# Thirteen turns of normed rows in the second pass: DMA transposes of two-byte halves in place of TensorE transposes

## The chip, the cores and the metric

One NeuronCore of a Trainium2 chip runs the whole kernel. The metric is the device time of one execution in microseconds (us); lower is better. The kernel before takes 807.27 us (median of three runs, 802.72 to 809.95).

## What is computed

Sixteen sequences x of 256 rows and 256 columns are updated by a gated cross-attention layer (a residual feed-forward network, a causal long convolution taken from a context, and a second feed-forward network) and then by a mixture of 16 experts on heads of 32 columns, two experts per head. Cut to what matters here:

```
y   = ffn(x_normed, W1a, W1b) * conv(context)        # "first pass", then the gate
xr  = ffn(y, W2a, W2b)                               # ffn(v) = silu(norm(v) @ Wa + ba) @ Wb + bb + v
x   = x + tanh(g_xattn) * xr                         # "second pass"
h   = norm(x) @ Wm + bm                              # heads
out = x + tanh(g_ffn) * (top2_experts(softmax(h @ E), h) @ Wo + bo)
```

## The kernel before

The 4,096 rows are eight blocks of 512 (b = 0 to 7); a block is a tile of 128 partitions by 1024 floats. Each engine has a program written out by hand, in which instructions run in order; they meet by semaphores alone. SyncE (SP) issues every DMA, in one queue, in program order. Products are made from f16 high and low parts (h, l), three products for one (`THREE`), into fp32 in PSUM.

A matrix product needs the columns of its rows on the partitions, so each block of normed rows is **turned** before use: eight TensorE transposes of 128x128 fp32 through the identity `ID` into two PSUM banks (`turn`, L554), then ScalarE rounds each bank to f16 into `XT[t % 2]["h"]` (L1427) and VectorE subtracts for the low part (`turn_lo`, L897). There are 24 turns: t = 0 to 7 of the first pass, `turn2(b)` of the gated rows and `turn3(b)` of the rows after the second network. `turn2(b)` for b of 2 and more uses `XT[0]`, `turn3(b)` for b up to 5 uses `XT[1]`.

The **second pass** is a loop over stages s = 0 to 7 in all programs. In stage s TensorE runs, in this order: `layer2` of block s-1 (50 matmuls, L590 and L598; its k-th quarter waits for the low part that GpSimd makes of the silu, L1610); `third_turn(s-2)`; `layer1` of block s (24 matmuls, L581); `logits` of block s-3 (L684); `heads` of block s-2 (12 matmuls, L673); `gated_turn(s+1)`. ScalarE runs the norm of block s-2 (`third_norm`, L1458 into DC), the norm of block s+1 (`gated_norm`, L1458 into `XN` in WK), the high part of turn3, eight silus (L1435, L1438), the high part of the heads (L1452) and the high part of turn2. VectorE makes the low parts, the norms' statistics (L914 to L940, which wait for a power by GpSimd, L1604), the residual sums (L1111, L1117: `second_out`), the logits less their maximum (L1128, L1131) and, in stages 4 to 7, fourteen steps that choose the experts of block 0 (`ROUTE0`).

SP's queue in a stage: one load of x (L333, which waits for `second_out` of block s-1), then `spread_heads(s-2)`: 12 DMAs of 64 KB that copy the heads to the layout of the experts (4 of the low part, L430, which wait for `heads_lo` of VectorE; 8 of the high part, L435). After stage 7 the experts' loop begins: 256 iterations to the end of the kernel. Its weights go to memory and come back (`keep_weights`, L447; `spread_weights`, L458), behind `spread_heads(5)` in SP's queue.

Of the kernel before, what the change touches and what calls it, by code (L numbers as in the profile page):

```python
# [64 lines left out]

def norm2(b):

    return 8 + b if b < 2 else 6 + 2 * b
# [21 lines left out]
def transposer_uses():  # L90

    out = [("conv", 0, 0), ("conv", 0, 1)]
    out += [("turn", turn2(s), k) for s in range(3) for k in range(2)]
    for s in range(2, NB):
        out += [("turn", turn3(s - 2), k) for k in range(2)]
        out += [("head", s - 2, g) for g in range(2)]
# [20 lines left out]
def flamingo_kernel(nc, xd, ctxT, peT, wp1, wp2, win, w1a, w1b, w2a, w2b, wm, wo,  # L117
                    ew1, ew2, eb, cols, rows, ident, ramp, tvec, ones, out):
    with ExitStack() as ctx:
# [79 lines left out]
        late_turns = [turn2(b) for b in range(3, NB)]  # L199

        def pt(kind, i, k):
            if kind == "turn" and i == 0:
                return PB[:, 512 * k:512 * k + 512]
            if kind == "turn" and i < NB:
                k += 0 if i < 5 else 2
                return PA[:, 512 * k:512 * k + 512]
            if kind == "turn" and i in late_turns:
                return PA[:, 512 * k:512 * k + 512]
# [51 lines left out]
        s_tl = [sem(f"s_tl{b}") for b in range(NB)]  # L260
        s_zx = [sem(f"s_zx{u}") for u in range(4)]
        s_out = [sem(f"s_out{u}") for u in range(2)]
        s_wt = [sem(f"s_wt{b}") for b in range(NB)]
# [9 lines left out]
        v_n3, v_hi, v_hh, v_cl = (sem("v_" + n) for n in ("n3", "hi", "hh", "cl"))  # L273
        a_exp, a_gelu = (sem("a_" + n) for n in ("exp", "gelu"))
# [15 lines left out]
        def pt_freed(kind, i, k):  # L290
            return {"turn": (v_lo, 2 * i + k + 1), "conv": (v_dc, NC),
# [5 lines left out]
        def xt_freed(t):  # L297
# [3 lines left out]
            for b in range(NB):  # L301
                if t == turn2(b):
                    return p_l1, 4 * (8 + b) + 4
                if t == turn3(b):
                    return p_head, 2 * b + 2

# [22 lines left out]
        def sync_program(sp):  # L329
# [107 lines left out]

            for s in range(NB):
                if s >= 1 and s + 1 < NB:
                    sp.wait_ge(v_out, 8 + s)  # L440
                    load_x(1, s + 1)
                if s >= 2:
                    spread_heads(s - 2)

            def keep_weights(b):
                sp.wait_ge(v_wt, b + 1)
                sp.dma_start(wtd.ap()[b, :, :], weighed(b)).then_inc(s_wt[b], 16)  # L447

            def spread_weights(m):
# [4 lines left out]
                if e == 0 and g == 0:  # L454
                    sp.wait_ge(s_wt[b], 16)
# [10 lines left out]
            keep_weights(0)  # L466
            for m in range(4):
# [20 lines left out]
        def tensor_program(pe):  # L488
# [51 lines left out]
            def turn(t, src):  # L540
                for k in range(2):
                    if t in late_turns:
                        bank = pt("turn", t, k)
                        pe.wait_ge(a_silu, 4 * (8 + late_turns.index(t) + 2) + k + 1)
                    elif t >= NB:
# [21 lines left out]
            def layer1(j, t, w):  # L567
                pe.wait_ge(v_lo, 2 * t + 2)
# [82 lines left out]
            def gated_turn(b):  # L651
                pe.wait_ge(a_n2, b + 1)
                turn(turn2(b), XN)

            def first_gated():
                gated_turn(0)
# [9 lines left out]
            def heads(b):  # L666
                t = turn3(b)
                xt = XT[t % 2]
                pe.wait_ge(v_lo, 2 * t + 2)
# [66 lines left out]
            for s in range(NB):  # L736
# [5 lines left out]
                if s >= 2:  # L742
# [1020 lines left out]
```

## Time and profile before

| what | value |
|---|---|
| median of three runs | 807.27 us |
| profiled execution, its span | 807.5 us |
| TensorE busy | 774.8 us, 96% |
| ScalarE busy | 670.3 us, 83% |
| VectorE busy | 531.4 us, 66% |
| GpSimd busy | 496.0 us, 61% |
| all DMAs | 117.06 MB, mean 145 GB/s |

The span is that of the one execution that was profiled; it lies 0.2 us above the median. A busy share is an average over stages that have different limits: the first pass ends near 190 us, the second pass near 300 us, and the rest is the experts' loop.

### The profile page before, as it was taken

How to read it: one execution, taken by the hardware profiler on the slowest of the kernel's cores; microseconds unless marked ns; L12 is line 12 of the kernel's file. 1: busy time of each engine (PE TensorE's matmuls, PEld its weight loads, DVE VectorE, ACT ScalarE, POOL GpSimd, SP SyncE). 2: the span in 40 equal slices, each digit the busy share in tenths (PEclk: the TensorE clock that was granted, in tenths of full speed). 3: DMA queues.
4: the chain of work that ended last, by engine and by line, in shares of the span. 5: the costliest groups of instructions: out<-in, count | busy, mean ns of one | idle time of the engine just before them, and what ended most of it. 6: DMA issues, size and time to landing. Idle time of an engine off the chain costs nothing.

```text
span 807.5 us, 23892 instructions
## 1 busy us (share of the span) xinstructions
PE 774.8 (96%) x9972; PEld 380.7 (47%) x9972; DVE 531.4 (66%) x988; ACT 670.3 (83%) x840; POOL 496.0 (61%) x389
## 2 busy tenths in 40 slices
PE   9999788889999998998999999999999999999997
PEld 4667455646676664333334434434434433434433
DVE  5999854557688985684665664764764764664445
ACT  4465854445869878799999999999999999999995
POOL 1374332027753542585787787787787787787674
PEclk9999999979999999999999999999999999999999
DMA  8990699941133316655465554555555555465552
GB/s 291 219 244 28 135 187 191 198 107 36 50 86 89 89 44 166 156 143 149 145 158 151 166 157 147 159 170 146 157 159 151 165 159 155 148 171 158 149 154 67
DMA packets 85971, 117.06 MB, mean 145 GB/s; under 512 B 13123, under 2 KB 65475, under 8 KB 85764
## 3 DMA queue, kind: packets, MB, share of 16 engines
q1 hardware_dynamic: 85864, 115.55, 55.2%
q8 instruction: 78, 1.28, 0.7%
q14 instruction: 29, 0.24, 0.1%
HBM read 101.28 MB, written 6.94 MB: 134 GB/s over the span
## 4 chain that ended last, share of the span: by engine, by line
PE 71%; DVE 10%; ACT 7%; SPq 5%; issue 3%; DMA 2%; POOL 2%; POOLq 0%; DVEq 0%; ACTq 0%
PE PB L792 26%; PE PA L780 18%; PE PT L780 9%; PE PA L581 5%; SPq L345 4%; PE PB L598 3%; PE PB L814 2%; PE PA L535 2%; DMA RA<-wpd 2%; DVE WK L897 2%; DVE SM L914 1%; ACT WK L1458 1%; PE PT L673 1%; ACT WK L1438 1%; ACT WK L1435 1%
## 5 line engine op out<-in xcount | busy, mean ns | idle before, releaser
L1677 POOL TENSOR_TENSOR WK<-WK 128x512 f32<-128x512 f32 x238 | 320.3, 1346 | 112.3 <-DVE WK L1333 102.2
L1582 ACT ACTIVATE WK<-PA 128x1024 f32<-128x1024 f32 x349 | 360.1, 1140 | 10.8 <-PE PA L780 10.3
L792 PE MATMUL PB<-WK,EW 128*32 128x512 f32 x2040 | 264.7, 594 | 0.4 <-DVE WK L1333 0.4
L780 PE MATMUL PA<-RA,EW 98*32 98x512 f16 x2800 | 201.6, 380 | 0.5 <-ACT WK L1582 0.5
L1582 ACT ACTIVATE WK<-PT 128x1024 f32<-128x1024 f32 x163 | 187.1, 1148 | 2.0 <-PE PT L780 1.7
L1610 POOL TENSOR_TENSOR WK<-WK 128x512 f16<-128x512 f32 x64 | 79.5, 1255 | 129.9 <-ACT WK L1438 128.6
L780 PEld LDWEIGHTS PA<-RA,EW 98*32 98x32 f16 x2800 | 68.1, 95 | 154.9 <-issue 80.4
L780 PE MATMUL PT<-RA,EW 98*32 98x512 f16 (+1 forms) x1312 | 99.6, 379 | 4.8 <-ACT WK L1582 3.4
L792 PEld LDWEIGHTS PB<-WK,EW 128*32 128x32 f32 x2040 | 62.4, 111 | 52.3 <-DVE WK L1333 0.9
L1333 DVE SCALAR_TENSOR_TENSOR WK<-PB,CV,W2h 128x512 f32<-128x512 f32 x64 | 48.1, 751 | 49.1 <-PE PB L792 49.1
L1333 DVE SCALAR_TENSOR_TENSOR WK<-PB,CV,W2l 128x512 f32<-128x512 f32 x63 | 47.3, 751 | 44.3 <-PE PB L792 44.3
L1333 DVE SCALAR_TENSOR_TENSOR WK<-PB,CV,DC 128x512 f32<-128x512 f32 x64 | 47.8, 748 | 37.1 <-PE PB L792 36.7
L780 PEld LDWEIGHTS PT<-RA,EW 98*32 98x32 f16 x1312 | 32.5, 95 | 76.9 <-issue 35.7
L1333 DVE SCALAR_TENSOR_TENSOR WK<-PB,CV,W1h 128x512 f32<-128x512 f32 x64 | 47.7, 746 | 29.0 <-PE PB L792 29.0
L1435 ACT ACTIVATE WK<-PA,CV 128x512 f16<-128x512 f32 x64 | 44.1, 690 | 24.6 <-PE PA L581 23.9
L1604 POOL TENSOR_TENSOR SM<-SM 128x4 f32<-128x4 f32 (+1 forms) x24 | 33.2, 1385 | 40.5 <-DVE SM L927 22.5
L1438 ACT ACTIVATE WK<-PA,CV 128x512 f32<-128x512 f32 x64 | 44.2, 690 | 0.0
L598 PE MATMUL PB<-W1h,WK 128*128 128x256 f16 x256 | 42.5, 273 | 1.0 <-issue 1.0
L598 PE MATMUL PB<-W2h,WK 128*128 128x256 f16 x256 | 42.5, 273 | 0.9 <-POOL WK L1610 0.9
L581 PE MATMUL PA<-WK,W1h 128*128 128x512 f16 x128 | 38.7, 384 | 0.0
L581 PE MATMUL PA<-WK,W2h 128*128 128x512 f16 x128 | 38.1, 379 | 0.0
L1080 DVE TENSOR_REDUCE DC<-PB 128x256 f32<-128x512 f32 x28 | 19.2, 691 | 26.6 <-PE PB L638 26.6
(220 smaller groups left out, 1086.8 us busy)
## 6 DMA issues: line engine op xcount, KB each, us to landing
RA<-wpd SPq DMA_DIRECT2D x128, 134.1 KB, 5.8
W1h<-wtd SPq DMA_DIRECT2D x128, 128.0 KB, 2.7
DC<-wtd SPq DMA_DIRECT2D x128, 128.0 KB, 2.8
W2h<-wtd SPq DMA_DIRECT2D x128, 128.0 KB, 2.7
W2l<-wtd SPq DMA_DIRECT2D x128, 128.0 KB, 2.7
WK<-in_x SPq DMA_DIRECT2D x15, 512.0 KB, 4.0
RA<-DC SPq DMA_DIRECT2D x96, 64.0 KB, 2.0
out<-WK SPq DMA_DIRECT2D x16, 256.0 KB, 2.8
```

The lines of the kernel that those rows point to most:

```text
L345: sp.dma_start(slot(c)[p0:p0 + K1, :, :, :].rearrange("p q i n -> p (q i) n"), src).then_inc(l_T[c % TR], 16)
L581: m = pe.matmul(pa, w[a][:, 512 * k + 128 * n:512 * k + 128 * n + 128], xt[b][:, 512 * k:512 * k + 512], start=(i == 0), stop=(i == 5))
L598: m = pe.matmul(o[t], S[b][:, 512 * k + 128 * t:512 * k + 128 * t + 128], w[a][:, 1024 + 256 * k:1024 + 256 * k + 256], start=False, stop= ...
L780: m = pe.matmul(pre(k)[32 * j:32 * j + 32, w * q:w * q + w], EW1[0:98, 128 * e + 32 * j:128 * e + 32 * j + 32], TS[0:98, h, t0:t0 + w], st ...
L792: m = pe.matmul(o[32 * q:32 * q + 32, :], EW2[:, 32 * e:32 * e + 32], hb[:, 512 * q:512 * q + 512], start=True, stop=True)
L1333: ve.scalar_tensor_tensor(out=dst, in0=po("down", n), scalar=col(C_B2 + e), in1=WB[n // 2 % 4][:, 512 * (n % 2):512 * (n % 2) + 512], op0= ...
L1435: ac.activation(S["h"][:, 512 * n:512 * n + 512], pa, ACT.Silu, scale=1.0 / SC, bias=col(bcol + n))
L1438: ac.activation(SF[n], pa, ACT.Silu, scale=1.0 / SC, bias=col(bcol + n)).then_inc(a_silu, 1)
L1582: ac.activation(HB[n % NH][:, 1024 * p:1024 * p + 1024], pre(k)[:, :], ACT.Gelu, scale=1.0 / (SC * SC)).then_inc(a_gelu, 1)
L1604: po_.tensor_tensor(SM[:, o:o + n], SM[:, o:o + n], SM[:, 6:7].broadcast_to([128, n]), ALU.pow).then_inc(g_pow, 1)
L1610: po_.tensor_tensor(sl, SF[n], sh, ALU.subtract).then_inc(g_slo, 1)
L1677: po_.tensor_tensor(AC[g], AC[g], PR[m % 3], ALU.add).then_inc(g_ac, 1)
```

## The change

Of the 24 turns, 13 go by another way: `turn2(1)` to `turn2(7)` and `turn3(0)` to `turn3(5)`. TensorE no longer transposes them. ScalarE rounds the normed rows themselves to f16 (`gated_hi` into `GN`, `third_hi` into `TN3`, 128x1024 each), VectorE subtracts for the low part (`gated_lo`, `third_lo`, 128x1024 each), and SP issues one `dma_start_transpose` of the 128 x 2048 two-byte elements (512 KB), which writes high and low parts of the turned block to `XT[t % 2]` (`turn_rows`). `layer1` and `heads` wait for that DMA's semaphore. The transpose waits on SP for the low part and for the last reader of that `XT`. VectorE's order changes with it, `third_norm(6)` moves behind `heads(5)` on ScalarE, and six semaphores are saved elsewhere (`s_wt`), which changes no order of work.

```diff
+        GN = WK[:, 5120:6144].bitcast(F16)
+        TN3 = W1["h"]
...
+            def turn_rows(t, rows, count, done):
+
+                sp.wait_ge(count, done)
+                sp.wait_ge(*xt_freed(t - 2))
+                both = WK[:, 3072 + 1024 * (t % 2):4096 + 1024 * (t % 2)].bitcast(F16)
+                sp.dma_start_transpose(both.rearrange("p (j n) -> p j n", n=128), rows[:, :]).then_inc(s_xt[t % 2], 16)
+
             for s in range(NB):
+                if s >= 2:
+                    turn_rows(turn3(s - 2), TN3, v_g3, s - 1)
                 if s >= 1 and s + 1 < NB:
                     sp.wait_ge(v_out, 8 + s)
                     load_x(1, s + 1)
+                if s + 1 < NB:
+                    turn_rows(turn2(s + 1), GN, v_g2, s + 1)
                 if s >= 2:
                     spread_heads(s - 2)
...
             def layer1(j, t, w):
-                pe.wait_ge(v_lo, 2 * t + 2)
+                if NB < t:
+                    pe.wait_ge(*turned(t))
+                else:
+                    pe.wait_ge(v_lo, 2 * t + 2)
                 xt = XT[t % 2]
...
-                if s >= 2:
-                    third_turn(s - 2)
...
-                if s + 1 < NB:
-                    gated_turn(s + 1)
...
+            def gated_lo(b):
+                ve.wait_ge(a_g2, b)
+                ve.tensor_tensor(by_halves(GN[:, 1024:2048]), XN.rearrange("p (t k c) -> p t k c", k=2, c=128),
+                                 by_halves(GN[:, 0:1024]), ALU.subtract).then_inc(v_g2, 1)
+
+            def third_lo(b):
+                ve.wait_ge(a_g3, b + 1)
+                ve.tensor_tensor(by_halves(TN3[:, 1024:2048]),
+                                 WSP[:, 1024 * b:1024 * b + 1024].rearrange("p (t k c) -> p t k c", k=2, c=128),
+                                 by_halves(TN3[:, 0:1024]), ALU.subtract).then_inc(v_g3, 1)
...
             for s in range(NB):
-                if s >= 1:
-                    turn_lo(turn2(s))
-                    if s + 1 < NB:
-                        gated_stats(s + 1)
-                        norm_shift(norm2(s + 1))
+                if 1 <= s < NB - 1:
+                    gated_stats(s + 1)
+                    norm_shift(norm2(s + 1))
                 for i in ROUTE0.get(s, ()):
                     route(0, i)
+                if s >= 2:
+                    third_lo(s - 2)
                 if s >= 1:
                     second_out(s - 1)
-                if s >= 2:
-                    turn_lo(turn3(s - 2))
-                if s >= 1:
                     third_stats(s - 1)
+                if s + 1 < NB:
+                    gated_lo(s + 1)
                 second_sum(s)
                 if s >= 3:
                     less_max(s - 3, PB[:, 0:512])
-                if s == 7:
-                    norm_shift(norm3(6))
+                if s >= 1:
+                    norm_shift(norm3(s - 1))
                 if s >= 2:
                     heads_lo(s - 2)
-                if 1 <= s < 7:
-                    norm_shift(norm3(s - 1))
...
+            def gated_hi(b):
+
+                if b == 1:
+                    ac.wait_ge(v_eb, 1)
+                else:
+                    ac.wait_ge(*turned(turn2(b - 1)))
+                ac.wait_ge(a_n2, b + 1)
+                split_rows(XN, GN[:, 0:1024], a_g2)
+
+            def third_hi(b):
+
+                if b:
+                    ac.wait_ge(*turned(turn3(b - 1)))
+                ac.wait_ge(a_n3, b + 1)
+                split_rows(WSP[:, 1024 * b:1024 * b + 1024], TN3[:, 0:1024], a_g3)
...
                 if s >= 2:
                     third_norm(s - 2)
+                    third_hi(s - 2)
                 if s == 5:
                     exp(0)
                     exp(1)
                 if s + 1 < NB:
                     gated_norm(s + 1)
-                if s >= 2:
-                    turn(turn3(s - 2))
+                    gated_hi(s + 1)
                 layer1(8 + s, C_B2A)
                 if s >= 2:
                     heads(s - 2)
-                if s + 1 < NB:
-                    turn(turn2(s + 1))
-                else:
-                    third_norm(6)
+            third_norm(6)
 
             def gelu(k):
                 n, p = divmod(k, 2)

```

Three places in the program show the new orders. First SP's queue around stage 4 (names in brackets are the semaphores waited for: v_hl and a_hh the heads' parts, v_g2 and v_g3 the low parts of the normed rows, p_l1 and p_head the last readers of `XT`). Before:

```order
L333 DMA WK<-in_x 128x4x256 [waits v_out]
L430 DMA RA<-DC 32x2x512 [waits v_hl]
L430 DMA RA<-DC 32x2x512 x3
L435 DMA RA<-DC 32x2x512 [waits a_hh]
L435 DMA RA<-DC 32x2x512 x7
```

Of the change:

```order
L444 DMA RA<-DC 32x2x512 [waits v_hl]
L444 DMA RA<-DC 32x2x512 x3
L449 DMA RA<-DC 32x2x512 [waits a_hh]
L449 DMA RA<-DC 32x2x512 x7
L457 DMA_TRANSPOSE WK<-W1h 128x16x128 [waits p_head,v_g3]
L347 DMA WK<-in_x 128x4x256 [waits v_out]
L457 DMA_TRANSPOSE WK<-WK 128x16x128 [waits p_l1,v_g2]
```

The transpose of block s-2 (source `TN3`, in W1h) stands behind the 12 DMAs of block s-3's heads; that of block s+1 (source `GN`, in WK) stands behind the load of x.

Second, VectorE in stage 4, from the experts' steps of the stage to the logits. Before:

```order
L1151 SCALAR_TENSOR_TENSOR W1l<-W1l,DC 128x512 [waits v_rt]
L1117 SCALAR_TENSOR_TENSOR XR<-PB,SM,WK 128x1024 [waits v_sum,p_l2]
L897 TENSOR_TENSOR WK<-PT,WK 128x512 [waits a_hi] x2
L914 BN_STATS SM<-XR 128x6 [waits a_n2,v_out]
L914 BN_STATS SM<-XR 128x6 x3
L921 BN_AGGR SM<-SM 128x2 [waits v_st]
L921 BN_AGGR SM<-SM 128x2 x3
L927 TENSOR_SCALAR SM<-SM 128x4 [waits v_ag]
L1111 SCALAR_TENSOR_TENSOR WK<-XR,SM,WK 128x1024 [waits l_x10]
```

Of the change:

```order
L1187 SCALAR_TENSOR_TENSOR W1l<-W1l,DC 128x512 [waits v_rt]
L931 TENSOR_TENSOR W1h<-DC,W1h 128x4x2x128 [waits a_g3]
L1153 SCALAR_TENSOR_TENSOR XR<-PB,SM,WK 128x1024 [waits v_sum,p_l2]
L950 BN_STATS SM<-XR 128x6 [waits a_n2,v_out]
L950 BN_STATS SM<-XR 128x6 x3
L957 BN_AGGR SM<-SM 128x2 [waits v_st]
L957 BN_AGGR SM<-SM 128x2 x3
L963 TENSOR_SCALAR SM<-SM 128x4 [waits v_ag]
L926 TENSOR_TENSOR WK<-WK 128x4x2x128 [waits a_g2]
L1147 SCALAR_TENSOR_TENSOR WK<-XR,SM,WK 128x1024 [waits l_x10]
```

The low part of turn3 moves ahead of `second_out`, and that of turn2 comes behind the statistics of the stage before instead of at the start of its own.

Third, TensorE between `layer2` and `layer1` of stage 5. Before, the end of `layer2`, turn3 and the first rows of `layer1`:

```order
L598 MATMUL PB<-W2h,WK 128x256 x2
L598 MATMUL PB<-W2l,WK 128x256
L554 MATMUL PT<-ID,DC 128x128 x8
L581 MATMUL PA<-WK,W2h 128x512 x2
L581 MATMUL PA<-WK,W2l 128x512
```

Of the change:

```order
L624 MATMUL PB<-W2h,WK 128x256 x2
L624 MATMUL PB<-W2l,WK 128x256
L607 MATMUL PA<-WK,W2h 128x512 x2
L607 MATMUL PA<-WK,W2l 128x512
L607 MATMUL PA<-WK,W2h 128x512 x2
```

The eight transposes are gone, here and behind `heads`; nothing takes their place on TensorE.

## Rows read from the trace of the kernel before

**Rows 1.** The page: span, TensorE's row, the chain that ended last.
```profile
span 807.5 us, 23892 instructions
PE 774.8 (96%) x9972; PEld 380.7 (47%) x9972; DVE 531.4 (66%) x988; ACT 670.3 (83%) x840; POOL 496.0 (61%) x389
PE 71%; DVE 10%; ACT 7%; SPq 5%; issue 3%; DMA 2%; POOL 2%; POOLq 0%; DVEq 0%; ACTq 0%
```
**Rows 2.** Windows of 16 us: from:to, length, engines' busy us, TensorE's clock, DMA share, GB/s.
```profile
236.00:252.00 16.00, 15.92 (x127) 10.96 (x128) 14.61 (x35) 11.73 (x23) 7.70 (x7) 1.00 0.31 84
268.00:284.00 16.00, 15.91 (x127) 10.73 (x124) 14.71 (x36) 12.52 (x24) 7.90 (x7) 1.00 0.32 83
```
**Rows 3.** Chain of waits from 236 to 300 us: start, us, engine, line; stage 7.
```profile
284.23 0.59 PE PB L590 x2
284.82 5.24 PE PB L598 x48
290.06 0.87 PE PT L554 x8
290.93 5.18 PE PA L581 x24
296.11 0.70 PE PB L684 x24
296.81 2.60 PE PT L673 x12
```
**Rows 4.** Timeline of TensorE: start, us, line, tiles, count; first `heads(0)`, last `heads(5)`.
```profile
216.20 0.38 PE L673 MATMUL PT<-WK,WMh 128*128 128x512 f16 x1
...
296.65 0.38 PE L673 MATMUL PT<-WK,WMh 128*128 128x512 f16 x1
```
**Rows 5.** Timeline of SP's queue, stages 3, 5 and 7 into the experts' loop.
```profile
229.75 0.59 SPq L333 DMA_DIRECT2D WK<-in_x  x1
...
253.11 2.51 SPq L430 DMA_DIRECT2D RA<-DC  x4
255.66 5.07 SPq L435 DMA_DIRECT2D RA<-DC  x8
260.77 0.59 SPq L333 DMA_DIRECT2D WK<-in_x  x1
...
300.94 2.50 SPq L430 DMA_DIRECT2D RA<-DC  x4
303.48 5.07 SPq L435 DMA_DIRECT2D RA<-DC  x8
308.59 0.58 SPq L447 DMA_DIRECT2D wtd<-DC  x1
```
**Rows 6.** DMA issues from 205 to 315 us: KB each, median us to landing.
```profile
RA<-DC SPq DMA_DIRECT2D x72, 64.0 KB, 2.0
WK<-in_x SPq DMA_DIRECT2D x5, 512.0 KB, 3.8
```
**Rows 7.** The page: DMA queue (packets, MB, share), slowest issue per byte.
```profile
q1 hardware_dynamic: 85864, 115.55, 55.2%
RA<-wpd SPq DMA_DIRECT2D x128, 134.1 KB, 5.8
```
**Rows 8.** Groups of instructions: busy us, mean ns of one, idle before.
```profile
L1072 DVE TENSOR_TENSOR RA<-DC,RA 128x1024 f16<-128x1024 f32 x4 | 5.7, 1456 | 0.8 <-ACT RA L1514 0.8
L1514 ACT ACTIVATE RA<-DC 128x1024 f16<-128x1024 f32 x4 | 4.1, 1054 | 5.8 <-DVE DC L1062 5.8
```
**Rows 9.** Timelines of ScalarE and VectorE: `third_norm(0)`; both turns' low parts in stage 5.
```profile
207.43 2.08 ACT L1458 ACTIVATE DC<-XR,SM 128x256 f32<-128x256 f32 x4 [0.96 <-DVE SM L940]
...
253.49 1.28 DVE L897 TENSOR_TENSOR WK<-PA,WK 128x512 f16<-128x512 f32 x2
...
260.67 1.29 DVE L897 TENSOR_TENSOR WK<-PT,WK 128x512 f16<-128x512 f32 x2 [0.90 <-ACT WK L1427]
```
**Rows 10.** Windows of 1 us, columns as in rows 2: clock around TensorE's idle times.
```profile
160.00:161.00 1.00, 0.33 (x25) 0.36 (x32) 0.40 (x1) 0.00 (x0) 0.00 (x0) 1.00 1.11 208
...
309.00:310.00 1.00, 0.00 (x0) 0.00 (x0) 1.00 (x2) 0.98 (x2) 0.00 (x0) 1.00 0.57 178
310.00:311.00 1.00, 0.82 (x3) 0.36 (x4) 1.00 (x4) 0.99 (x2) 0.00 (x0) 0.76 0.40 150
311.00:312.00 1.00, 1.00 (x4) 0.30 (x3) 0.93 (x7) 1.00 (x2) 0.00 (x0) 0.50 0.12 33
```
**Rows 11.** Timeline of TensorE: an idle time of 1.0 us; `heads(6)` from its first matmul on.
```profile
160.67 0.63 PE L624 MATMUL PT<-RA 60*32 60x256 f16 x32 [1.00 <-DMA RA<-wpd]
...
310.18 0.73 PE L673 MATMUL PT<-WK,WMh 128*128 128x512 f16 x2 [1.73 <-DVE WK L897]
...
314.56 0.61 PE L780 MATMUL PA<-RA,EW 98*32 98x512 f16 x8
```

More of the change, by code:

```diff
@@ L63, in turn3, with by_tensor, by_transfer @@
     return norm3(b)
+def by_tensor(t):
+    return (*range(NB), turn2(0), 22, 23).index(t)
+def by_transfer(t):
+    ts = [turn2(b) for b in range(1, NB)] + [turn3(b) for b in range(6)]
+    return sorted(u for u in ts if u % 2 == t % 2).index(t)
 def norm2(b):
@@ L92, in transposer_uses @@
     out = [("conv", 0, 0), ("conv", 0, 1)]
[L93 to L96, printed above, removed]
+    out += [("turn", turn2(0), k) for k in range(2)]
+    out += [("head", b, g) for b in range(6) for g in range(2)]
     out += [("wt", 0, 0), ("turn", 22, 0), ("turn", 22, 1), ("head", 6, 0), ("head", 6, 1),
@@ L197, in flamingo_kernel @@
         po_at = {u: i for i, u in enumerate(po_list)}
-        late_turns = [turn2(b) for b in range(3, NB)]
+        GN = WK[:, 5120:6144].bitcast(F16)
+        TN3 = W1["h"]
         def pt(kind, i, k):
@@ L205, in pt @@
                 k += 0 if i < 5 else 2
-                return PA[:, 512 * k:512 * k + 512]
-            if kind == "turn" and i in late_turns:
                 return PA[:, 512 * k:512 * k + 512]
@@ L260, in flamingo_kernel @@
         s_tl = [sem(f"s_tl{b}") for b in range(NB)]
+        s_xt = [sem(f"s_xt{i}") for i in range(2)]
         s_zx = [sem(f"s_zx{u}") for u in range(4)]
         s_out = [sem(f"s_out{u}") for u in range(2)]
-        s_wt = [sem(f"s_wt{b}") for b in range(NB)]
+        s_wt = [sem(f"s_wt{i}") for i in range(2)]
         l_wb = [sem(f"l_wb{i}") for i in range(4)]
@@ L273, in flamingo_kernel @@
         v_n3, v_hi, v_hh, v_cl = (sem("v_" + n) for n in ("n3", "hi", "hh", "cl"))
+        a_g2, a_g3, v_g2, v_g3 = (sem(n) for n in ("a_g2", "a_g3", "v_g2", "v_g3"))
         a_exp, a_gelu = (sem("a_" + n) for n in ("exp", "gelu"))
@@ L290, in pt_freed @@
         def pt_freed(kind, i, k):
-            return {"turn": (v_lo, 2 * i + k + 1), "conv": (v_dc, NC),
+            return {"turn": (v_lo, 2 * by_tensor(i if kind == "turn" else 0) + k + 1), "conv": (v_dc, NC),
                     "head": (v_hl, 2 * i + k + 1), "wt": (v_wt, 1)}[kind]
@@ L466, in sync_program @@
             keep_weights(0)
+            sp.wait_ge(*turned(turn3(5)))
             for m in range(4):
@@ L541, in turn @@
                 for k in range(2):
[L542 to L545, printed above, removed]
+                    if t >= NB:
                         bank = take_pt("turn", t, k)
@@ L649, in convs @@
                         flip(c, s)
-            def gated_turn(b):
-                pe.wait_ge(a_n2, b + 1)
-                turn(turn2(b), XN)
             def first_gated():
-                gated_turn(0)
+                pe.wait_ge(a_n2, 1)
+                turn(turn2(0), XN)
             def third_turn(b):
@@ L668, in heads @@
                 xt = XT[t % 2]
[L669 removed]
+                if b < 6:
+                    pe.wait_ge(*turned(t))
+                else:
+                    pe.wait_ge(v_lo, 2 * by_tensor(t) + 2)
                 for g in range(2):
```

25 lines of the change are left out of this document (19 added, 6 removed).

## Prediction

> **What bounds the kernel now.** I read the page first, then the windows of the second pass, then the chain of waits and the queue of SP. The page shows TensorE busy for 96% of the span and the largest part, 71%, of the chain that ended last [rows 1]. That is a mean; the change touches only the second pass, 190 to 300 us. There too TensorE is full: 15.9 of 16 us in the windows of stages 4 and 6, at the full clock, with VectorE close behind at 14.6 and 14.7 us [rows 2]. The chain of waits gives the parts of a stage: `layer2` from 284.23 to 290.06, turn3 0.87, `layer1` 5.18, `logits` 0.70, `heads` 2.60 us [rows 3]. `heads(0)` starts at 216.20 and `heads(5)` at 296.65 us [rows 4], so a stage lasts 80.45/5 = 16.09 us. Without its two turns TensorE's own work in a stage is 5.83 + 5.18 + 0.70 + 2.60 = 14.3 us.
>
> What a reader misses by looking at the engines alone is SP. `spread_heads` holds its queue for 2.51 + 5.07 us, 0.63 us for each of 12 DMAs [rows 5]. Before, nobody in the second pass waits for what stands behind them. After, the transpose of turn3 does.
>
> **What the change removes.** 13 turns of 0.87 us [rows 3] are 11.3 us of TensorE, the most that there is to gain. On ScalarE two pairs of roundings per stage go and two roundings of 128x1024 come, 1.05 us each by the nearest row [rows 8]; on VectorE two low parts of 1.28 us [rows 9] are replaced by two of 128x1024 from SBUF, 1.46 us by the nearest row [rows 8], so +0.36 us a stage. Below nothing is excluded for both, as no row has less for that size. ScalarE has 11.7 and 12.5 of 16 us busy [rows 2], which hides its part; VectorE's 14.7 + 0.4 us fit into a stage of 16 us but not into one of 14.3.
>
> **The DMA transpose** has no row. It moves 512 KB. Its cost from issue to landing, D, is bounded from below by the 2.0 us in which the small SBUF copies of 64 KB land, and by 3.8 us for the load of x with the same 512 KB [rows 6]; nothing suggests that transposing is cheaper than copying, so less than 2.0 is excluded. From above, the slowest bytes of the trace are the loads from wpd, 134.1 KB in 5.8 us [rows 7], or 22 us for 512 KB. Between them: its source falls into 128 x 16 = 2,048 pieces of 256 bytes, 128 for each of 16 engines; the mean packet took 0.552 x 16 x 807.5 / 85,864 = 0.083 us [rows 7], so 10.6 us, with the 2.0 us of a small copy 12.6. I take D = 4.2 us, near the load of the same bytes with a tenth more, because packets there too are mostly small and still land in 3.8.
>
> The Trainium skill (DMA: Bandwidth & Descriptors, Latency and other measured facts) gives a DMA transpose an effective 261 GB/s. By it the 512 KB would take 2.0 us, with the 2.0 us of the small copy an estimate of 4.0 us; no row here shows a transpose.
>
> **Where the transposes land.** turn2(s+1) is issued when `layer1` of stage s has ended and the low part is there, some 11 to 14 us into the stage, and is needed by the next `layer1`, 16.2 + 5.8 = 22 us in. It has 8 us for D, and for the load of x ahead of it in the rings, 3.8 us: hidden. That cover is gone only from D of about 8 us on.
>
> turn3(s-2) is another matter. The heads of the block before have to end, be rounded and be spread before SP comes to it: `heads(5)` starts at 296.65 [rows 4] and SP is free at 303.48 + 5.07 = 308.55 us [rows 5], 11.9 us later. (That stage has the least VectorE work; stage 5 has its SP free at 260.73.) Then D, and `heads` can start. So the change makes a loop that was not there: **heads, heads' parts, 12 DMA issues, transpose, heads**, of 11.9 + D + 0.1 for semaphores. With D = 4.2 that is 16.2 us, against 16.09 before and 14.3 of TensorE's work: the two turns' 1.74 us come back as an idle time of 1.9 us before every `heads`. Behind the waiting `heads` stand the next `layer2` and with it VectorE's and ScalarE's stage, so the whole pass goes at the loop's pace. Behind the waiting transpose on SP stand the load of x, turn2 and the next spread; they have the slack given above.
>
> The first of them: `third_norm(0)` starts at 207.43 and takes 2.08 us [rows 9], then 1.05 and 1.46 [rows 8], D, and 0.3 for four semaphores: 216.5 us, where `heads(0)` started at 216.20. So +0.3, and the turns saved ahead of it are lost there. Five periods add 5 x 0.1 = 0.5 us. What follows `heads(5)` (its spread, the weights through memory, the experts' loop) starts that much later, with nothing in between to absorb it.
>
> **The clock.** Six times TensorE will now sit idle for some 1.9 us. The trace shows what may follow: after an idle time of 1.73 us before `heads(6)` the granted clock falls from 1.00 to 0.50, from 2.4 to 1.2 GHz [rows 10], and these 12 matmuls take from 310.18 to 314.56, 4.38 us in place of 2.60 [rows 11, 3]. An idle time of 1.00 us at 160 us left the clock at 1.00 [rows 10, 11]. `heads` is in the loop, so each fall costs 1.8 us. All six falls would be 10.7 us, none would be 0; with few rows to tell I take half of them, 5.4 us.
>
> **The sum**, against the profiled execution: 807.5 + 0.3 + 0.5 + 5.4 = 813.7 us; the median shown is 0.2 below that execution. I say 814 us.
>
> **Rivals.**
> - *The loop without the clock* (17%): D near 4 and no fall. 808 us. For it: heads' idle times sit in a busy stretch, unlike the two in the trace. Even with a shorter D not much is gained, because VectorE then holds stages 4 and 6: 14.7 + 0.4 us busy and about 1 us of waiting for GpSimd.
> - *Transposes priced by pieces* (17%): D of 5 to 13 us. At 12.6 the loop is 24.6 us, 8.5 longer: 6 x 8.5 = 51, with six falls 62, so 869 us; at D = 7 it is 6 x 2.9 + 10.7 = 28 more, 836 us. Against it: x's packets are small too. For it: a transposed write lies scattered over all partitions.
> - *Linear at the slowest rate* (6%): D = 22 us, the loop 34 us, 6 x 17.9 + 10.7 = 118 more, 925 us, and more if the stage's two transposes run one behind the other.
> - *Faster* (5%): D is 2.0 us like the small copies, the loop 14.0, so TensorE never waits and the stage is 14.3 us. Five stages give 5 x 1.8 = 9 and the first `heads` 1.9 us, 11 in all and 796.6 us; with VectorE holding two stages at 16 us, 800 us. It decides at D of 2.3 us, where loop and TensorE's work are equal; a gain of 1% needs about that.
>
> The Trainium skill (VectorE: DVE Perf Modes, The three transpose paths) gives a two-byte 128x128 square 1309 ns by DMA. An estimate by it for 16 squares in a row is 21 us, which would be the fourth case, some 920 us. No row here bears it out.
>
> **How the numbers follow.** The likeliest case, the loop with some falls of the clock, has 55% and a range of its own of 806 to 822 us. A change of about 1%, 8 us, is what a measurement of this kernel can tell from none. Faster by more than 1%: most of the fourth rival, 4%. Slower by more than 1%: half of the likeliest case (27%), and the second and third rivals (23%), 50 to 51%. Within 1%: the rest, 45%. The range of 803 to 842 us leaves out the faster case below, and above it D beyond some 8 us.
>
> **What would show it.** In the profile after: eight rows of L554's kind per removed turn gone; an idle time of about 1.9 us before each `heads` from `heads(1)` on, released by a DMA; `heads` to `heads` 16 to 17 us; the transposes of turn3 issued right behind the last DMA of the spread; the time from issue to landing near 4.2 us; falls of the clock at some of these places; no wait before `layer1`. I am wrong if D is far from 4, if `heads` waits for VectorE's low part and not for SP's queue, or if `layer1` is what waits.

## The result and the profile after

The changed kernel takes 828.7 us (median of four runs, 824.65 to 829.28) against 808.3 us of the kernel before (four runs, 802.72 to 809.95): 1.0243 times as long, 95% interval 1.0197 to 1.0289. Its profiled execution has a span of 826.5 us, where that of before has 807.5, so 19.0 us are to be found. The page of the changed kernel, span, busy times, packets and the chain that ended last:

```profile
span 826.5 us, 23671 instructions
PE 772.4 (93%) x9868; PEld 369.7 (45%) x9868; DVE 532.9 (64%) x975; ACT 671.8 (81%) x827; POOL 496.6 (60%) x389
DMA packets 113012, 123.89 MB, mean 150 GB/s; under 512 B 40163, under 2 KB 92515, under 8 KB 112804
PE 69%; SPq 8%; DMA 6%; DVE 6%; ACT 3%; issue 3%; POOL 2%; POOLq 0%; DVEq 0%; ACTq 0%
```

TensorE has 2.4 us less to do than before and a share of 93% in place of 96% [rows 1]; SP's queue and the DMAs have larger shares of the chain, 8% and 6% where they had 5% and 2%. The marks of the second pass show where (columns of the windows: from:to, length, busy time and instructions of each engine, granted clock, DMA share, GB/s). Kernel before, from the first `layer1` to `heads(0)`, from there to `heads(5)`, and the rest:

```profile
185.40:216.20 30.80, 29.93 (x199) 19.24 (x197) 21.02 (x47) 21.36 (x40) 21.64 (x15) 1.00 0.19 52
216.20:296.65 80.45, 79.76 (x632) 54.39 (x632) 70.73 (x162) 64.78 (x116) 41.80 (x32) 1.00 0.30 78
296.65:807.50 510.85, 498.09 (x7148) 199.19 (x7144) 307.68 (x456) 487.86 (x533) 370.36 (x291) 0.99 0.53 150
```

The changed kernel, between the same marks:

```profile
185.50:220.10 34.60, 27.72 (x174) 16.38 (x172) 24.42 (x54) 24.02 (x41) 22.74 (x16) 1.00 0.51 81
220.10:312.80 92.70, 76.59 (x551) 47.15 (x552) 71.92 (x145) 64.09 (x104) 45.02 (x35) 0.94 0.59 128
312.80:826.50 513.70, 499.59 (x7142) 197.51 (x7142) 305.25 (x453) 487.19 (x531) 366.70 (x288) 0.99 0.53 150
```

Of the 19.0 us, 3.8 lie ahead of `heads(0)`, 12.2 in the five periods (18.5 us each, before 16.1) and 2.9 behind `heads(5)`. In the middle part TensorE's busy time falls by only 3.2 us: ten turns of 0.87 go, 8.7, and three falls of the clock take 5.2 back. Its idle time grows from 0.7 to 16.1 us. The waits of the second pass, 188 to 335 us (engine and line, releaser, us in total, times, longest), name it:

```profile
PE PT L699 <- DMA WK<-W1h: 16.1, 5, 4.5
DVE WK L1366 <- DMA W1h<-wtd: 4.5, 1, 4.5
PE PB L624 <- POOL WK L1665: 4.4, 3, 2.2
```

`WK<-W1h` is the transpose of turn3, L699 is `heads`. These are the waits before `heads(1)` to `heads(5)`; before `heads(0)` TensorE sat idle for 2.29 us, for which the profile names no releaser, but its transpose was issued at 215.71 us, 4.4 us ahead of it. The transposes of turn2 (`WK<-WK`) cost `layer1` one wait of 0.23 us. The chain of waits of the changed kernel around `heads(4)` and `heads(5)` (start, us, what) is the loop itself. The same view of the kernel before, from 216 to 297 us, has neither a DMA nor SP's queue in it:

```profile
289.29 4.33 DMA WK<-W1h
...
293.67 4.40 PE PT L699 x12
...
298.10 0.70 ACT DC L1485
...
298.82 0.76 DVE DC L1055
...
299.60 0.60 SPq L444
...
306.63 0.60 SPq L449
...
307.33 5.39 DMA WK<-W1h
...
312.77 4.09 PE PT L699 x12
```

`heads` takes 4.40 us, not 2.60, because the granted clock is down. Windows of the changed kernel around three `heads`; the clock is the third value from the end:

```profile
257.00:261.00 4.00, 3.05 (x15) 1.41 (x16) 3.42 (x5) 0.94 (x2) 2.69 (x3) 1.00 1.00 236
276.00:280.00 4.00, 4.00 (x12) 1.47 (x11) 1.86 (x2) 1.38 (x3) 2.29 (x3) 0.57 0.91 227
293.00:297.00 4.00, 3.33 (x8) 1.19 (x9) 2.59 (x4) 0.55 (x1) 2.60 (x3) 0.57 1.02 226
```

Four of the six `heads`, at 238.90, 275.30, 293.67 and 312.77 us, ran mostly at half the clock (4.46, 4.17, 4.40 and 4.09 us) after idle times of 4.49, 3.04, 2.37 and 3.16 us. Those at 220.11 and 257.95 us kept it, after 2.29 and 3.04 us.

### The profile page after: what moved, and what is told of

Its sections match the earlier page's. It is cut to its first block, busy times and chain, and to the rows that moved or that the text cites. A ratio compares the mean times of both kernels' runs of the same rounds, so it can differ in the third digit from the quotient of the medians.

```text
span 826.5 us, 23671 instructions
## 1 busy us (share of the span) xinstructions
PE 772.4 (93%) x9868; PEld 369.7 (45%) x9868; DVE 532.9 (64%) x975; ACT 671.8 (81%) x827; POOL 496.6 (60%) x389
## 2 busy tenths in 40 slices
DMA packets 113012, 123.89 MB, mean 150 GB/s; under 512 B 40163, under 2 KB 92515, under 8 KB 112804
## 4 chain that ended last, share of the span: by engine, by line
PE 69%; SPq 8%; DMA 6%; DVE 6%; ACT 3%; issue 3%; POOL 2%; POOLq 0%; DVEq 0%; ACTq 0%
PE PB L814 25%; PE PA L802 17%; PE PT L802 8%; PE PA L607 5%; SPq L449 4%; PE PB L624 3%; DMA WK<-W1h 3%; PE PT L699 3%; PE PB L836 2%; SPq L359 2%; SPq L444 2%; PE PA L561 2%; DMA RA<-wpd 2%; POOL WK L1665 1%; ACT WK L1491 1%
## 5 line engine op out<-in xcount | busy, mean ns | idle before, releaser
L1665 POOL TENSOR_TENSOR WK<-WK 128x512 f16<-128x512 f32 x64 | 82.6, 1304 | 136.6 <-ACT WK L1471 135.2
L1659 POOL TENSOR_TENSOR SM<-SM 128x4 f32<-128x4 f32 (+1 forms) x24 | 31.2, 1299 | 48.8 <-DVE SM L963 31.4
L699 PE MATMUL PT<-WK,WMh 128*128 128x512 f16 x64 | 23.6, 457 | 19.8 <-DMA WK<-W1h 16.1
## 6 DMA issues: line engine op xcount, KB each, us to landing
WK<-in_x SPq DMA_DIRECT2D x15, 512.0 KB, 5.1
```

What stands on the lines that cost most here:

```text
L699: m = pe.matmul(bank, WM[a][:, 256 * k + 128 * g:256 * k + 128 * g + 128], xt[bb][:, 512 * k:512 * k + 512], start=(i == 0), stop=(i == 5))
L1665: po_.tensor_tensor(sl, SF[n], sh, ALU.subtract).then_inc(g_slo, 1)
```

## Experiments

Single profiles differ by several us ahead of the second pass (its first `layer1` starts between 181.3 and 189.2 us). So all are read by the same marks, in us: from that start to `heads(0)`, the five periods to `heads(5)`, and the rest. The time and the ratio come from the timed runs beside the kernel before.

| kernel | time | ratio, 95% interval | to heads(0) | five periods | rest |
|---|---|---|---|---|---|
| before | 808.3 | 1 | 30.8 | 80.4 | 510.9 |
| changed | 828.7 | 1.024 (1.020 to 1.029) | 34.6 | 92.7 | 513.7 |
| x1 | 813.8 | 1.006 (1.005 to 1.008) | 34.8 | 80.0 | 512.7 |
| x2 | 822.1 | 1.016 (1.012 to 1.021) | 34.3 | 88.0 | 512.2 |
| x3 | 818.3 | 1.011 (1.007 to 1.014) | 32.3 | 88.0 | 511.2 |
| x4 | 821.0 | 1.016 (1.012 to 1.020) | 34.7 | 88.9 | 511.6 |
| x6 | 818.0 | 1.013 (1.009 to 1.017) | 33.7 | 87.4 | 512.8 |
| x7 | 820.3 | 1.015 (1.010 to 1.019) | 34.1 | 87.0 | 512.8 |
| x8 | 814.2 | 1.006 (1.003 to 1.009) | 34.6 | 80.7 | 510.3 |
| x9 | 809.7 | 1.002 (1.000 to 1.005) | 32.6 | 79.0 | 510.8 |
| x10 | 859.7 | 1.067 (1.062 to 1.071) | 33.8 | 126.4 | 512.0 |
| x11 | 821.9 | 1.019 (1.014 to 1.025) | 35.1 | 90.1 | 509.8 |
| x12 | 817.4 | 1.013 (1.009 to 1.017) | 33.9 | 86.7 | 512.9 |
| x13 | 831.1 | 1.029 (1.025 to 1.033) | 34.5 | 96.0 | 513.8 |

### x1: the spread of the heads behind the transpose

```diff
             for s in range(NB):
                 if s >= 2:
                     turn_rows(turn3(s - 2), TN3, v_g3, s - 1)
+                if s >= 3:
+                    spread_lo(s - 3)
                 if s >= 1 and s + 1 < NB:
                     sp.wait_ge(v_out, 8 + s)
                     load_x(1, s + 1)
                 if s + 1 < NB:
                     turn_rows(turn2(s + 1), GN, v_g2, s + 1)
-                if s >= 2:
-                    spread_heads(s - 2)
+                if s >= 3:
+                    spread_hi(s - 3)
+            spread_heads(5)
```

`spread_lo` and `spread_hi` are the four and the eight DMAs of `spread_heads`; ScalarE's `exp(0)` and `exp(1)` go behind `heads` of stage 5.

> The changed kernel with one order on SP's queue turned round: the transpose of turn3(s-2) is issued ahead of the 12 DMAs that spread the heads of block s-3 (its four low-part DMAs come right behind it, the eight high-part ones behind the transpose of turn2), and two exponentials of stage 5 move behind the silus so that they don't wait for the later spread. Theory (the loop heads, 12 DMA issues, transpose, heads sets the pace): the transpose is issued some 4 to 5 us earlier in a stage, when VectorE's low part is there; idle time before heads falls from 2.4-4.5 us to below 1.5, the clock falls less often, a stage goes from 18.5 to 15.5-16.5 us, and the time is 808 to 815 us. Rival (the chain norm, rounding, low part on ScalarE and VectorE is what comes last, SP's queue only seems to be): idle time before heads stays near 3 us and the time stays above 823 us.

813.8 us, in the expected range; the five periods are 80.0 us, 16.0 each, and the wait before `heads` is 4.6 us in all in place of 16.1:

```profile
PE PT L709 <- DMA WK<-W1h: 4.6, 3, 2.3
```

All thirteen turns are still DMA transposes. The order of SP's queue (with the two exponentials, whose part was not measured by itself) was worth 12.7 us in the five periods and 14.9 of time: the loop through the twelve issues is shown. What x1 lacks against the kernel before lies ahead of `heads(0)` (4.0) and behind `heads(5)` (1.8). TensorE has 8.7 us less to do in the five periods, and they are still no shorter than 80.0. In its profile 4.6 us are the waits left for transposes, and `heads(0)`, at half clock, takes 1.8 us more. One of these waits, of 1.06 us before `heads(3)`, still comes through SP's queue: the chain reaches that transpose through the issue of turn2's (3.46 us) and eight DMAs of the spread. So x1 does not show by itself that VectorE holds the stage.

### x4: TensorE kept busy while it waits

```diff
+                    for _ in range(10):
+                        pe.matmul(PB[:, 512:1024], ON[:, 0:128], ON[:, :], start=True, stop=True)
```

These matmuls stand ahead of `heads` from the second on; nobody uses their products.

> The changed kernel with ten matmuls of 512 columns on ones, whose result nobody reads, put between logits and heads in stages 3 to 7 (about 2.2 us of work in an idle time of 2.4 to 4.5 us). Theory of the clock (its falls to 1.2 GHz at heads lengthen the loop by 1.5 to 1.8 us each, in four of six stages): the clock stays at 2.4 GHz, heads take 2.6 us, the time falls by 5 to 8 us to 820-823 us. Rival (heads at half clock cost nothing, or the clock falls anyway): 827 to 830 us.

821.0 us. In its windows the granted clock stays at 1.00 where the changed kernel's was 0.57:

```profile
276.00:282.00 6.00, 5.57 (x30) 2.72 (x29) 3.42 (x6) 5.20 (x9) 5.51 (x5) 1.00 1.05 227
293.00:298.00 5.00, 4.34 (x21) 1.82 (x20) 4.54 (x6) 1.25 (x2) 4.06 (x3) 1.00 1.03 226
```

The fall at `heads(1)` remained (2.32 us idle, 0.60 in the window of 242 to 246 us); the other three are gone. In the changed kernel these three made `heads` last 4.17, 4.40 and 4.09 us in place of 2.60, 4.9 us in all; in x4 the periods shrink by 3.8 us and the rest by 2.1. Work that nobody needs makes the kernel 7.7 us faster: the falls of the clock, in a loop through `heads`, are shown. The times give a little more than the marks, and the two intervals of the ratio touch at 1.020, so the 7.7 us are known to a few us only; the windows and the lengths of `heads` carry the proof.

### x3 and x2: one of the two sets of turns by DMA

x3 puts turn2 back on TensorE, ScalarE and VectorE as before and keeps turn3 by DMA; x2 does the reverse.

> The other part alone: only the six turns of turn3 go by DMA, the seven of turn2 are back on TensorE. Theory of the loop: the loop is untouched and the turns of turn2 fall into TensorE's idle times; a stage stays at 17.5-18.5 us; the first two stages get back the 2 to 4 us that ScalarE's rounding ahead of the silus took: 820 to 827 us. Rival (turn2's transposes, which hold SP's queue for 3.5 us each, are a large part of the loss): below 815 us.

818.3 us, a little under what was expected. `heads(0)` comes 2.3 us earlier than in the changed kernel, and the periods are 17.6 us instead of 18.5: the loop is there with turn3's transposes alone, while SP no longer issues those of turn2 in the same stage. Of the 12.2 us that the periods of the changed kernel are too long, 4.7 go with turn2's transposes and the orders around them. Part of that is the clock: in x3 two `heads` of the periods ran mostly at half clock (`heads(0)`, 4.03 us, and `heads(4)`, 4.45 us), in the changed kernel three.

> One part of the change alone: only the seven turns of turn2 go by DMA, the six of turn3 are back on TensorE. Theory of the loop: no matmul of heads waits for a DMA, turn2's transposes stay hidden (11 us of slack), the stage is TensorE's or VectorE's, 15.2-16.0 us; less 7 x 0.87 = 6 us of transposes, plus some 2 to 3 us that the rounding ahead of the silus costs in the first two stages: 802 to 808 us, no slower than before. Rival (the transposes disturb everything that shares the DMA rings or SP's queue, whichever turn they are for): 815 us or more.

822.1 us: a miss of 14 us and more. The waits of x2 (L615 begins `layer2` and waits for `less_max`, L917 is the low part of turn3):

```profile
PE PB L615 <- DVE DC L1165: 8.2, 4, 3.7
DVE WK L917 <- ACT WK L1459: 7.9, 4, 2.6
```

No wait for a transpose is among them; they are hidden. VectorE waits for ScalarE, which in x2 rounds the gated rows (L1506) before turn3's banks, and TensorE waits for VectorE. That is an order of my own making, not the kernel's.

### x7: x2 with ScalarE's two roundings exchanged

```diff
                 if s + 1 < NB:
                     gated_norm(s + 1)
-                    gated_hi(s + 1)
+                    if s < 2:
+                        gated_hi(s + 1)
                 if s >= 2:
                     turn(turn3(s - 2))
+                    if s + 1 < NB:
+                        gated_hi(s + 1)
```

> As x2_turn2_only, with ScalarE's rounding of the third norm's rows put ahead of its rounding of the gated rows, where x2 had it behind. x2 lost 14 us, and VectorE waited there 7.9 us for that rounding. Theory (x2's loss was that order, not the second norm's transposes): VectorE's waits at the low parts (L917) go, PE's waits at L615 go back under 2 us, periods return to about 16.1 us, what is left is the later heads(0) of 2 to 3 us, and the kernel takes 806 to 813 us. Rival (six more transposes by the rings cost this much in any order): 818 to 824 us.

820.3 us, another miss:

```profile
PE PB L615 <- DVE DC L1165: 6.9, 4, 3.7
```

`DVE WK L917 <- ACT` has left the list's head, the wait for `less_max` has not. The exchange took 1.0 us off the periods and 1.9 us off the time, less than the intervals can tell from nothing: ScalarE's order was a small part of x2's loss at most. In x7's chain, VectorE stands at most pieces from 223 to 257 us: its order, arranged for rows that come from SBUF, now also carries turn3's low parts from PSUM. Whether that order is the whole of it was not settled.

### x6: a copy in place of the transpose

```diff
-                sp.dma_start_transpose(both.rearrange("p (j n) -> p j n", n=128), rows[:, :]).then_inc(s_xt[t % 2], 16)
+                sp.dma_start(both, rows[:, :]).then_inc(s_xt[t % 2], 16)
```

> The changed kernel with each of its thirteen transposes replaced by a plain copy of the same 512 KB between the same two tensors, so the second pass's turned rows are not turned (that part of the computation is left out). It separates the transposing from the bytes and from the order of the queue. In the changed kernel a transpose lands 4.3 to 4.4 us after its issue where heads(b) waits, and SyncE's issue is held 1.6 to 2.0 us by it. Theory (the period of 18.5 us is a loop over SyncE's twelve issues, the row's transfer and heads, whatever kind the transfer is): the copy lands 3.8 to 4.2 us after its issue, SyncE is held about 0.6 us, heads(b) still waits over 1.5 us in every stage, and the kernel takes 820 to 828 us. Rival (the transposing itself is the cost, by its small packets that hold the rings): the copy lands in about 2.5 us, the waits before heads shrink under 1 us, the load of x goes back from 4.8 to 3.8 us, and the kernel takes 812 us or less.

818.0 us, between the two. Issues at L457 (ns: min, median, max), in x6:

```profile
L457 SPq DMA_DIRECT2D WK<-W1h x6: 472/543/547, 211.7 to 298.8; - x6
DMA to landing us min/median/max: 3.1/3.3/3.6
```

and in the changed kernel:

```profile
L457 SPq DMA_TRANSPOSE WK<-WK x7: 1855/3525/5799, 190.8 to 292.4; - x7
L457 SPq DMA_TRANSPOSE WK<-W1h x6: 1616/1878/2008, 215.7 to 307.3; - x6
```

(The landing row of x6 is that of turn3's six copies alone.) Turning costs about 1.0 us of landing on the loop's path and 1.3 us of SP. The periods shrink by 5.2 us: the five landings take 16.9 us in all in place of 22.8, and the rest of the loop is 0.7 us longer. The waits before `heads` remain, 11.7 us in all: with the transposing left out, the loop still stands. The marks explain 7.1 of the 10.7 us of time; the remainder lies ahead of the second pass, where single profiles differ anyway.

### x8 and x9: the queue put right for the rest, and turn2 on TensorE

x8 is x1 with the first two weight loads ahead of the last eight DMAs of the spread; x9 is x8 with turn2 on TensorE, as in x3.

```diff
-            spread_heads(5)
...
+            spread_lo(5)
             keep_weights(0)
             sp.wait_ge(*turned(turn3(5)))
-            for m in range(4):
-                if m == 2:
-                    sp.wait_ge(p_l2, 16)
+            for m in range(2):
+                spread_weights(m)
+            spread_hi(5)
+            sp.wait_ge(p_l2, 16)
+            for m in range(2, 4):
                 spread_weights(m)
```

> As x1_spread_behind, with the experts' first two weight loads issued ahead of the second half of the last spread. In x1 the first of these weights land late (VectorE waited 5.1 us for them, PE 0.56 and 1.68). Theory (x1's remaining loss against the kernel before is the late heads(0), 2 to 3 us, and this pile of issues, 2 to 3 us): 810 to 812 us, VectorE's wait for the weights under 2.5 us. Rival (the weights' landing is covered and x1's loss lies elsewhere): 813 to 814 us as in x1.

The wait for the weights goes (x1 had `DVE WK L1376 <- DMA W1h<-wtd` at 5.1 us) and the part behind `heads(5)` shrinks by 2.4 us in the profile, to what it was before. The timed median, 814.2 us, shows none of it: with x1's 813.8 the intervals overlap. So that gain is seen in one profile and not in the times.

> Only the third norm's rows by transpose, the second norm's by TensorE, with the spread of the heads' rows behind the transpose and the load of x as in x1, and the first weights ahead as in x8. Theory (two separate costs add: x3's rows of the second norm on TensorE keep heads(0) early, and the order of the queue opens the loop): periods of 16.0 to 16.4 us, heads(0) at about 217, the kernel at 804 to 810 us, level with the kernel before or a little faster. Rival (the removed TensorE work is worth nothing because VectorE and GpSimd hold the period at 16): 811 to 815 us.

809.7 us, ratio 1.0021 (0.9996 to 1.0047): level with the kernel before, in the expected range. Six turns are off TensorE and the periods are 79.0 us, 0.3 less each than before; `heads(0)` is 1.8 us later, since the first transpose still takes its 4.4. TensorE's whole idle time in the periods, 3.6 us, is two waits for a transpose, before `heads(2)` and `heads(4)`. In the chain each of these transposes starts straight behind VectorE's low part of turn3 (L947, 1.23 and 1.14 us) and not behind SP's queue. That low part comes late behind the norm (VectorE, GpSimd, ScalarE) in the one case and behind the experts' steps on VectorE in the other: with the queue put right, this is what keeps `heads` waiting. This is the best version with a DMA transpose in it, and it does not beat the kernel before.

### x10 and x12: turn2's transposes with the engines' old orders

In x10 ScalarE rounds behind the silus, VectorE makes the low part at the start of the next stage, and SP issues the transpose there, which is behind the spread. x12 moves the issue ahead of the spread:

```diff
             for s in range(NB):
-                if s >= 1:
-                    turn_rows(turn2(s), GN, v_g2, s)
                 if s >= 1 and s + 1 < NB:
                     sp.wait_ge(v_out, 8 + s)
                     load_x(1, s + 1)
+                if s + 1 < NB:
+                    turn_rows(turn2(s + 1), GN, v_g2, s + 1)
                 if s >= 2:
                     spread_heads(s - 2)
```

> Only the second norm's rows by transpose, with the orders of VectorE and ScalarE as in the kernel before: ScalarE rounds the gated rows behind layer one's silus, VectorE makes their low parts at the start of the next stage, where it made those of TensorE's transposes, and the transpose is issued there. x2 and x7 (the same turns by transpose, but with the changed kernel's orders) took 822 and 820 us with PE waiting 7 to 8 us for less_max. Theory (x2's and x7's loss is the engines' order, not the transposes; it is also what makes heads(0) late): heads(0) starts at most 32 us after layer one of the second pass begins (before 30.8, changed kernel 34.6), the five periods are 79 to 82 us, PE waits under 2 us for less_max, and the kernel takes 803 to 810 us. Rival (seven more transposes cost by themselves, or land too late for layer one, about 10 us after heads began): PE waits over 1 us a stage for WK<-WK, and the kernel takes 814 us or more.

859.7 us. Its chain of waits shows the same kind of loop, made longer by a `layer1`:

```profile
232.53 4.38 DMA WK<-WK
...
236.96 7.95 PE PA L606 x24
244.91 0.70 PE PB L706 x24
245.61 2.60 PE PT L695 x12
...
248.24 0.69 ACT DC L1486
...
248.96 0.76 DVE DC L1053
...
249.73 0.60 SPq L446
...
257.58 0.60 SPq L451
...
258.28 4.36 DMA WK<-WK
```

From transpose to transpose 25.75 us, and `layer1` at 7.95 us in place of 5.18 [rows 3]: after idle times of about 8 us the clock was down too. I had not seen this loop when I wrote down what to expect, though it is the one of the prediction.

> As x10, with the transpose of the second norm's rows issued ahead of the spread of the heads' rows where x10 issued it behind. x10 took 860 us in a loop of 24.9 us: heads, its parts 1.5, twelve issues 7.6, transpose 4.4, layer one 8.0, head bias 0.7. Theory (the loop closes through SyncE's twelve issues, as in the changed kernel): without them a transpose is issued about 2.7 us after heads ends (rounding on ScalarE is done before, VectorE's heads parts 0.7 and low parts 1.2) and lands 4.4 us later, before layer one wants it; the waits for WK<-WK fall from 35 us to under 4 us in all, and the kernel takes 803 to 811 us. Rival (the low parts at the start of the stage come too late by themselves): WK<-WK is still waited for 2 us or more a stage and the kernel takes 816 us or more.

The waits for turn2's transposes fall from 43.1 us (x10, seven waits) to 10.2 us and the time by 42 us:

```profile
PE PA L606 <- DMA WK<-WK: 10.2, 7, 2.3
```

With the clock that falls in their wake, twelve issues of 0.63 us cost 42 us in x10: its loop is shown. But 817.4 us is outside the 803 to 811 I expected, and two of the waits of 2.3 us are as the rival had them. From `heads` at 235.18 to the landing of the next transpose at 244.92 it is 9.7 us, and TensorE's work until then is 2.60 + 5.83 + 0.87 = 9.3 us [rows 3]: the old place of the low parts leaves no room for 4.4 us of transpose.

### x11 and x13: all thirteen, in these orders

x11 is x8 with x10's orders; x13 issues turn2's transpose ahead of `spread_hi`.

> All thirteen turns by transpose, with the second norm's in the orders of x10 and the spread and the weights ordered as in x8. Theory (three separate costs of the changed kernel are undone: the loop over the spread, the early rounding, the late weights): heads(0) 33 to 34 us after layer one begins (the transpose of the third norm's rows is still waited for there), five periods 79 to 82 us, the kernel 805 to 812 us. Rival (two transposes a stage on one queue hold each other up once both are wanted within one stage): PE waits for WK<-W1h grow over x8's 5.3 us, and the kernel takes 814 us or more, as x8.

> As x11, with the transpose of the second norm's rows issued ahead of the second half of the spread (eight issues, 5.1 us) where x11 issued it behind. Theory (x11's waits of 1.4 to 3.9 us a stage for WK<-WK are these eight issues): those waits fall under 1 us a stage, and the kernel takes 808 to 815 us. Rival (putting the spread off by a transpose makes the gathered rows late for the routes, or two transposes collide): 818 us or more.

821.9 and 831.1 us, both misses. In x11 `layer1` waits 15.6 us in all for turn2's transposes, as they are ready later. In x13 that is still 13.1, so the eight issues were not what these waits came from, and the spread put off makes others late; its waits:

```profile
PE PA L619 <- DMA WK<-WK: 13.1, 7, 3.8
DVE DC L1179 <- DMA RA<-DC: 10.6, 4, 3.5
PE PT L711 <- DMA WK<-W1h: 8.0, 4, 3.2
```

VectorE waits for the spread heads, and `heads` waits 8.0 us for turn3's rows, where x11 has 0.9; that the first makes the second was not shown by itself. The changed kernel's own early rounding, which costs time in stages 0 and 1 (below), was the better place in the rest of the pass.

## Why the prediction was right, and where its sum fell short

The sign, the mechanism and the range held: 828.7 us in 803 to 842. The likeliest case's own range, 806 to 822, did not hold it. The forecast was 814, so nearly 15 us are missing from the sum. Slower by more than 1% had been given only even chances, so the sign alone is no great merit.

Nearly 2 us of the 15 are one of bookkeeping: the sum starts from the span of 807.5 us and is read as a time, 0.2 us above the median. In every run on record the time is 1.8 to 2.3 us longer than the span. Span against span, 813.7 us stand against 826.5, and the 12.8 us between them are found below: 3.5 ahead of `heads(0)`, 4.9 of late issues, 1.8 of D, 1.3 of clock and 1.4 behind `heads(5)`, together 12.9.

**The transpose, D.** Predicted 4.2 us; measured 4.3 to 4.4 us in four turns of the loop and 5.39 in the last. The price by pieces (12.6) and the linear one (22) are ruled out. The load of x with the same bytes [rows 6] gave nearly the right size, but partly by luck: x6 shows that 3.3 us are the copy and 1.0 the turning, and not 3.8 and a tenth. Nor does the size hold for every transpose: turn2's, which follow the load of x, took 5.6 us in the median. The Trainium skill's rate (DMA: Bandwidth & Descriptors, Latency and other measured facts) gave an estimate of 4.0 us, near what turn3's transposes took. The Trainium skill's 1309 ns per square (VectorE: DVE Perf Modes, The three transpose paths) gave an estimate of 21 us for 16 squares in a row, which the trace contradicts.

**The loop.** Right in kind (x1), with the idle time before `heads(1)` to `heads(5)` released by a DMA. From the start of `heads` to the issue of the transpose I took 11.9 us from stage 7. It measured 14.41, 14.63, 12.95, 13.99 and 13.66 us, 13.9 in the mean. Three of these hold a `heads` at half clock, 5.2 us together, which stood in the sum as its own term. The other 4.9 us in five periods were not in it: after `heads(0)` VectorE came to the heads' parts only at 225.21 us, behind a wait for GpSimd's statistics, which gives the 14.41; and single issues of the spread took 1.1 to 1.5 us in place of 0.6 (at 247.20, 266.11 and 288.02 us). x6 has such issues too (1.68 us at 278.53), so it is not the turning; what it is no run isolated. I took the stage with the least VectorE work and an empty queue as the measure of all. The trace of the kernel before had the others: after `heads(0)`, which started at 216.20 us [rows 4], the spread's last eight issues are

```profile
224.64 5.07 SPq L435 DMA_DIRECT2D RA<-DC  x8
```

so SP was free only 13.5 us after `heads` had started. For `heads(1)` to `heads(4)` it was 13.0, 12.2, 12.4 and 12.8 us. With the mean of these five, 12.8, the sum would have been 4.4 us longer.

**The clock.** Predicted three falls of six, 5.4 us, a number half way between none and all; there were four, 6.7 us with the one of `heads(5)`. x4 confirms the term.

The five periods then: 0.5 predicted from the loop, 5.2 for three falls, 4.9 for the late issues and 1.8 for D make 12.4, of 12.2 measured.

**heads(0).** Predicted +0.3, measured +3.8. The term is wrong in its starting point: `third_norm(0)` starts at 209.85, where I left it at 207.43 [rows 9]. The chain of the changed kernel in the stage before goes through ScalarE and GpSimd:

```profile
199.91 2.09 ACT WK L1491 x4
...
202.08 0.04 ACT WK L1506
202.12 0.92 issue
203.04 0.67 ACT WK L1468
203.71 0.59 ACT WK L1471
204.30 0.07 issue
204.37 3.35 POOL WK L1665 x2
207.71 0.97 POOL SM L1659
```

In the kernel before GpSimd started the same low parts earlier, by its chain:

```profile
202.11 3.18 POOL WK L1610 x2
```

ScalarE now rounds the gated rows (L1506, 0.96 us of the chain) ahead of the silus, and does so in stages 0 and 1: 2.3 us later in GpSimd, 2.4 in `third_norm(0)`. I had called ScalarE's part hidden because 4 of 16 us were free; a mean share does not show that in two stages the rounding stands in the chain. The other 1.2 us are VectorE, which comes to `third_lo(0)` at 214.46, not at 213.0, behind a wait of 1.12 us for GpSimd's statistics. x3, without this rounding, has 2.3 us less here. Moving the rounding behind the silus (x10) brought no earlier `heads(0)` than 33.8 us: `layer1` then waited 1.91 us for the transpose.

**Behind heads(5).** I wrote that it starts later by the same amount. It grew by 2.9 us: the last `heads` at half clock, 1.5, and the first weights. SP's queue brought them 4.5 us after VectorE wanted them.

**Hidden parts.** The transposes of turn2 were hidden, as forecast (0.23 us waited). The gain of 11.3 us of TensorE was given back in full: x1 has it and its periods shorten by only 0.4 us in all; x9 has a part of it and shows 0.3 us a stage, the rest going into two waits for a transpose (3.6 us).

## What to carry to other kernels

Before a step goes from an engine to a DMA, follow what its issue stands behind in the queue: if the last thing ahead of it waits for the result that the transfer feeds, a loop is closed. Its length is the sum of all that stands in it: here `heads`, its parts, twelve issues of 0.63 us and one landing of 4.3 us, so the number of issues weighs more than the bytes. Price such a loop by the mean of all the stages that the trace shows, not by the cleanest one, and count the half clock of the work behind each wait as part of the loop. A step that is put ahead of others on an engine with a low share still costs its full length wherever that engine is in the chain of a stage.

## What the runs showed of the hardware

- A DMA transpose of 128 x 2048 two-byte elements (512 KB) from SBUF to SBUF lands 4.3 to 4.4 us after its issue (turn3's in the changed kernel, 5.39 us once), a plain copy of the same bytes 3.3 us (x6). Those of turn2, issued behind the load of x, take 5.6 us in the median (copies in x6 4.0), the first of all 7.8 us; in x10 and x12, where the load of x is not issued right ahead of them, 4.4 us. From 185 to 335 us of the changed kernel:

```profile
WK<-WK SPq DMA_TRANSPOSE x7, 5.6
```

- The transpose holds SP's queue for 1.6 to 2.0 us, and for 3.4 to 3.8 us when it is issued right behind the load of x (2.9 us once, after a gap of 1.4 us), 5.8 us once, for the first of all. A copy holds it 0.5 us in the median. Everything behind it on SP waits as long.
- It makes small packets: those under 512 bytes go from 13,123 to 40,163, in x6 they are 13,331. The row of the kernel before:

```profile
DMA packets 85971, 117.06 MB, mean 145 GB/s; under 512 B 13123, under 2 KB 65475, under 8 KB 85764
```

- Idle times of 2.3 to 4.5 us in an otherwise busy stretch took the granted clock to half in four of six cases. An idle time of 3.04 us did it once and once not. The same 2.29 us before `heads(0)` kept the clock up in the changed kernel and was followed by a `heads` of 4.43 us in x1; 1.73 us before `heads(6)` halved it in the kernel before [rows 10], and 1.74 us in x10 did not (`heads(6)` 2.77 us). So the length of the idle time alone does not tell. With ten unneeded matmuls in the gap and 0.4 to 0.8 us of idle time left the clock stayed at 1.00.
